# Layer 3 of a graph network: one more wait between groups of gathers on GpSimd

## What is computed

```python
h = (x @ W).reshape(N, H, C)
a_src = jnp.sum(h * att_src, axis=-1)
a_dst = jnp.sum(h * att_dst, axis=-1)
logits = a_src[src] + a_dst[dst]
logits = jnp.where(logits > 0, logits, NEG_SLOPE * logits)
seg_max = jax.ops.segment_max(logits, dst, num_segments=N)
e = jnp.exp(logits - seg_max[dst])
denom = jax.ops.segment_sum(e, dst, num_segments=N)
alpha = e / (denom[dst] + EPS)
msgs = h[src] * alpha[:, :, None]
out = jax.ops.segment_sum(msgs, dst, num_segments=N)
```

## Time and profile before

| | us |
|---|---|
| median of 3 runs | 6218.11 |
| lowest and highest | 6216.2, 6225.41 |
| the profiled execution | 6181.86 |
| its span, first to last instruction | 6180.0 |
| of it, from the first gather of layer 3 to the last | about 3823 to 6123 |
| layer 3's gathers, busy time on GpSimd | 1539.4 in 1612 |

### The profile page before, as it was taken

How to read it: one execution, slowest core, us unless ns; L and a number is a source line. 1 busy time by engine, 2 the same in 40 slices (tenths; PEclk the granted TensorE clock), 3 DMA queues, 4 the chain that set the end, 5 groups by cost and what they waited for, 6 DMA issues and landing times.

```text
span 6180.0 us, 70833 instructions
## 1 busy us (share of the span) xinstructions
PE 4521.5 (73%) x24017; PEld 3636.4 (59%) x24017; DVE 2509.1 (41%) x8563; ACT 1745.2 (28%) x3903; POOL 3125.5 (51%) x3324
## 2 busy tenths in 40 slices
PE   6999978889899899998998997234443444434445
PEld 5888865666666666666668996234343443434434
DVE  8999952333333333333335443123222222222324
ACT  5888841222222222222224553001110111101111
POOL 0000026666666666666650002666666666666664
PEclk9999989999999999999999998566666656666666
DMA  6777765555555555555546885222222222222221
GB/s 153 163 164 166 165 161 180 181 180 182 184 179 182 177 183 178 180 184 177 182 152 196 243 243 156 47 48 50 49 48 50 48 49 50 50 48 49 50 49 34
DMA packets 472464, 804.79 MB, mean 130 GB/s; under 512 B 72608, under 2 KB 301131, under 8 KB 462123
## 3 DMA queue, kind: packets, MB, share of 16 engines
q0 software_dynamic: 140192, 443.73, 28.9%
q1 hardware_dynamic: 317802, 346.76, 17.7%
q10 hardware_dynamic: 14112, 9.74, 0.5%
HBM read 663.72 MB, written 136.22 MB: 129 GB/s over the span
## 4 chain that ended last, share of the span: by engine, by line
PE 54%; another core or an unknown queue 24%; issue 9%; DVE 9%; DMA 2%; ACT 1%; POOL 0%; DVEq 0%; ACTq 0%; SPq 0%
PE bank L1028 17%; PE bank L1015 12%; PE bank L1197 7%; PE bank L682 5%; PE bank L662 2%; DVE ring L1335 2%; DMA atab<-at 2%; PE bank L1548 2%; PE bank L583 1%; DVE hs L631 1%; PE bank L964 1%; DVE hs L629 1%; DVE tops L1285 1%; PE bank L1528 0%
## 5 line engine op out<-in xcount | busy, mean ns | idle before, releaser
L543 POOL DMA_INDIRECT ring<-ptab,src x1612 | 1526.6, 947 | 829.4 <-issue 446.2
L543 POOL DMA_INDIRECT ring<-htab,src x1612 | 1539.4, 955 | 772.4 <-issue 465.4
L1028 PE MATMUL bank<-ring,oh 128*126 128x384 f32 x3224 | 1280.0, 509 | 80.8 <-issue 76.9
L981 DVE TENSOR_TENSOR ring<-bank,ring 128x512 f32<-128x512 f32 x806 | 540.3, 687 | 1588.6 <-remote 715.7
L1548 PE MATMUL bank<-ring,oh 128*126 128x132 f32 x3224 | 689.0, 348 | 552.4 <-issue 546.4
L1015 PE MATMUL bank<-w1e,ea 128*128 128x256 f32 x3224 | 896.8, 397 | 117.4 <-issue 89.0
L1548 PEld LDWEIGHTS bank<-ring,oh 128*126 128x126 f32 x3224 | 593.8, 249 | 622.4 <-issue 611.2
L1015 PEld LDWEIGHTS bank<-w1e,ea 128*128 128x128 f32 x3224 | 627.6, 198 | 393.1 <-issue 167.7
L1028 PEld LDWEIGHTS bank<-ring,oh 128*126 128x126 f32 x3224 | 624.4, 197 | 361.5 <-issue 155.6
L997 ACT ACTIVATE ring<-ring 128x1024 f32<-128x1024 f32 x403 | 425.4, 1056 | 1224.4 <-DVE ring L981 875.1
L682 PE MATMUL bank<-xhl,at 128*126 128x258 f32 x3822 | 712.4, 323 | 0.0
(11 more groups left out here) (271 smaller groups left out, 4466.9 us busy)
## 6 DMA issues: line engine op xcount, KB each, us to landing
atab<-at POOLq DMA_DIRECT2D x78, 1543.5 KB, 9.9
ring<-ea_r SPq DMA_DIRECT2D x403, 256.0 KB
ea<-ea_t SPq DMA_DIRECT2D x403, 256.0 KB
adjb<-atab SPq DMA_DIRECT2D x156, 535.5 KB, 4.7
adjb<-atab SPq DMA_DIRECT2D x78, 472.5 KB, 4.4
ring<-ptab,src POOLq DMA_INDIRECT x1612
ring<-htab,src POOLq DMA_INDIRECT x1612
ptab<-pO ACTq DMA_DIRECT2D x49, 128.0 KB, 7.3
```

Source lines behind the costliest of these rows:

```text
L543: return e.indirect_dma_start(o, None, table, bass.IndirectOffsetOnAxis(ap=src[:, t:t + 1], axis=0))
L981: e.tensor_tensor(group1(gi, m % 2), MLP[m % NM][:, :].rearrange("p (g f) -> p g f", g=2), group1(gi, m % 2), ALU.add).then_inc(s_edge, 1)
L1028: w = e.matmul(SUM[s % 2][0:SL, 0:384], slots_of(s, i), rv1[:, t // G % NR1, t % G, :], start=i == 0, stop=t == END[s])
```

## The change

In `pool3`, before the gathers of every group but the first, GpSimd waits until all gathers of the group before have landed. The wait on `s_sum3` stays behind it.

```diff
--- before.py
+++ after.py
@@ -1248,6 +1248,8 @@
             def pool3(e):
                 e.wait_ge(s_htab, 16 * NB)
                 for s in range(NS):
+                    if s:
+                        e.wait_ge(*landed3(s - 1))
                     for i in range(SIZE[s]):
                         if s >= NR3 and i % CH == 0:
                             e.wait_ge(s_sum3, chunk(s - NR3, i))
```

## The result

The changed kernel takes 6236.81 us (median of 9 runs, 6225.41 to 6247.56), the kernel before 6216.2 us (9 runs beside them). The ratio is 1.0029, with a 95% interval of 1.0021 to 1.0038: slower by 20.6 us, where no change was forecast. It lies inside the range 6204 to 6266, but on the side to which 0.27 were given.

A forecast was written before the change was run, and what follows sets the result against it. In layer 3 GpSimd's gathers were taken to stretch TensorE's rounds, which hold GpSimd back at the ring. Exposed waits, at most 46 us, were expected back at later ring waits: sum 0, forecast 6218 us, range 6204 to 6266.

The forecast's parts named there:

- the side to which 0.27 were given: Whole kernel: the chance of 0.27 that the change makes it slower by over 0.2% (12 us).
- How many are exposed: Layer 3 group boundaries: 38 hidden behind a ring wait at cost 0, 38 exposed, 34 of these after the ring's filling.
- The exposed wait: GpSimd at a group's first gather: landing after 1.64 us against the usual 0.30, so at most 1.34 us added.
- That TensorE uses a pause wherever it stands: Layer 3 gathers: an exposed 1.34 us comes back at the next ring wait, so the change costs 0.
- the small pause of group 9: Evidence in the earlier trace: 0.46 us extra at its 8th gather shortened the wait at the 15th by 0.41.
- The third rival: Layer 3: TensorE's own 30 us a group binds, GpSimd's slack absorbs the waits, 6218 us again; chance 0.15.
- That gathers hold TensorE up: Layer 3: TensorE's round of about 10 us is stretched to 30 while GpSimd issues gathers.
- Rival 1: Exposed boundary waits: a short pause lets nothing through, later ring waits keep their length, +46 us, 6264; chance 0.24.
- Its extreme of 103 us: All 77 boundaries pay 1.34 us because the covered ones lose their cover, 6321 us; chance 0.03 beyond.
- Rival 2: Group boundaries: the added pause breaks the gather run, TensorE falls behind less, -34 us, 6184; chance 0.12.
- The forecast of 1.3 to 1.7 us at every first gather: Sign in the profile after: that much idle or more before each group's first gather, where 0.30 stood at 38.
- a constant idle total near 760 us: Sign on layer 3's gather line: idle stays near 465 + 295 us, some 40 us moving to the boundaries.

The follow-up runs named there:

- Experiment 13: The changed kernel with its two waits in the other order, s_sum3 first, then the landing; slow chip, 6222.62 against 6223.86 us, ratio 0.9997.
- experiment 15: Kernel before plus a long-true wait on s_htab ahead of each chunk's ring wait, no landing wait; slow chip, 6259.04 against 6223.86 us, ratio 1.0051.
- experiment 7: Kernel before with layer 3's gathers left out, SyncE bringing rows by one plain transfer a group, GpSimd storing; slow chip, 4579.68 us, one run.
- experiments 10 and 11: Kernel before plus landing waits at the 15th gather, or at the 1st and 8th; slow chip, 6187.39 (0.9998) and 6190.29 (1.0001) against 6190.28 us.

## Why the prediction was wrong

- **The step that failed** is in "How many are exposed": "There the data has landed before the ring slot is free: the new wait costs 0, and its cover is the ring wait." The landing is indeed hidden there, but the wait is not free. It takes the place on the gather that the ring wait had, the ring wait becomes an instruction of its own, and the gather starts 0.5 us later after each release. With 28, 31 and 36 ring waits left at the boundaries that makes 14 to 18 us; measured were 20.6, 15.4 and 14.5 us in the three comparisons on slow chips. Experiment 13 takes the restart away and the cost goes, experiment 15 makes twice as many and the cost doubles. I had looked for what an additional wait hides behind, and not at what it does to the instruction that it stands before.
- **The exposed wait** was priced at 1.34 us from ScalarE's start after the landing and measured 1.56; 43 rather than 34 were exposed, since the ring waits moved.
- **That TensorE uses a pause wherever it stands**, for which I took 0, held. One pause at the 15th gather at ratio 0.9998 and two pauses a group at 1.0001, with the same sum of idle time, bear it out; the small pause of group 9, a single case, pointed the right way. The third rival, TensorE's own pace of 30 us, could have given the same times, but without the gathers layer 3 takes 738 us: it is refuted.
- **That gathers hold TensorE up** was right for the slow chips: the earlier trace rows and experiment 7. The page of the Trainium skill (SBUF — State Buffer, "Who interferes with whom"), by which TensorE waits for no other engine, does not account for the slow chips (2300 us with gathers, 738 without); on the quick chips, where GpSimd's issue is the bound, no run tests it. By what path it happens is open: no run here shows it.
- **Rival 1** (short pauses lost, +46 us) gave the right sign for the wrong reason; experiments 10 and 11 refute it. Its extreme of 103 us, every boundary paying, has its like on the quick chip, +115.7 us, but for another reason: there GpSimd's issue is the bound, and nothing gives a pause back.
- **Rival 2** (faster) did not come: no kernel with pauses was quicker than before beyond the noise.
- The forecast of 1.3 to 1.7 us at every first gather came out as 1.78 us or more at all 77. That of a constant idle total near 760 us came out as 782 in the first profile of the change, and as 772 against 756 on one chip.

## What to carry to other kernels

A wait that is hidden behind a longer one is not free if both stand ahead of the same instruction: here the order of two lines decided whether the instruction started 0.26 or 0.76 us after the release that mattered. In these kernels the gather carried the wait that is written first, and the one written second became the instruction of its own. So write the wait that is released last first, and look in the trace which of the two the instruction carries and how long after the release it starts, not only at the length of the wait. And ask of every pause who else lives on it: the same 1.56 us pauses were free where another engine needed them and cost their full length where the waiting engine was the bound.

## What was not expected of the hardware

The same kernel takes 5568 us on some chips and 6186 to 6225 on others, 11% apart, and the difference lies in the stages in which GpSimd gathers: in layer 3, for example, 2357 us against some 2090 us, but 737 and 738 us without gathers on one chip of each kind. In the first profile before, on a slow chip, VectorE's line 1285 waits 629.0 us in 53 waits whose releaser the profile calls remote (the earlier trace rows show one). In that trace many of TensorE's matmuls are recorded long before their semaphores are raised, those of line 1530 by some 20 us in many groups, and the raises come close together while GpSimd stands still: in the wait before group 23 at 2.4, 3.8, 3.9 and 4.0 us after its last gather. Of 513 raises by TensorE in layer 3, 210 fall into the ring waits of over 2.3 us, which are 280 of 2299 us. On the quick chip, in the kernel of experiment 1, the same line (1287 there) waits 175.1 us in all, in 74 waits, each time for TensorE's matmul itself. Its rows:

```profile
L1287 DVE TENSOR_TENSOR tops<-bank,away x78: 690/692/694, 3508.5 to 5520.1; 126x512 f32<-126x512 f32 x78
...
  PE bank L1532: 175.1, 74
```

What makes the chips differ stays open.
